# Transposed features in a ring of three 128-sample tiles: the next block's dense-table items around and between the second tile's products

## What is computed

```
e = stack([tbl_f[ids[:, f]] for f in range(26)], axis=1)   # 2048 x 26 x 128
c = concatenate([e, dense[:, None, :]], axis=1)            # 2048 x 27 x 128
z = einsum('bfd,bgd->bfg', c, c)[:, triu_i, triu_j]        # 351 pairs each
h = concatenate([z, dense], axis=1)                        # 2048 x 479
h = maximum(h @ W1 + b1, 0); h = maximum(h @ W2 + b2, 0)   # 512, then 256
y = h @ W3                                                 # 2048 x 1
```

## Time and profile before

| what | value |
|---|---|
| median of the three runs | 480.82 us |
| profiled execution, its own time | 486.82 us |
| its span, first to last instruction | 485.0 us |
| TensorE matmul / weight load busy | 437.1 us / 413.9 us |
| VectorE, ScalarE, GpSimd busy | 310.4, 230.2, 247.8 us |
| mean granted TensorE clock | 0.975 |

### The profile page before, as it was taken

The page is one execution under the profiler, slowest core; times in us unless marked ns, Lnnn a source line. Parts: engine busy times, 40 slices in busy tenths (PEclk is TensorE's granted clock), DMA queues, the critical chain, the costliest instruction groups (busy, mean ns, idle before and its releaser), DMA issues.

```text
span 485.0 us, 9121 instructions
## 1 busy us (share of the span) xinstructions
PE 437.1 (90%) x3464; PEld 413.9 (85%) x3464; DVE 310.4 (64%) x503; ACT 230.2 (47%) x731; POOL 247.8 (51%) x264
## 2 busy tenths in 40 slices
PE   1776669899998999999889999999999999999978
PEld 1665669899897999999889998989898989889966
DVE  4998237875387735885469645885488745882441
ACT  2643343644455453644545444644546453634643
POOL 3652665655655556455654656555565556461000
PEclk9999679999999999999999999999999999999999
DMA  6789212322123312232122321232133312310000
GB/s 229 222 258 160 57 45 58 81 70 72 48 63 75 81 51 57 70 82 73 44 66 78 73 65 55 70 76 78 39 72 80 80 55 56 72 49 18 1 1 0
DMA packets 23995, 36.20 MB, mean 75 GB/s; under 512 B 6185, under 2 KB 18097, under 8 KB 23952
## 3 DMA queue, kind: packets, MB, share of 16 engines
q1 hardware_dynamic: 14880, 18.03, 14.7%
q0 software_dynamic: 8192, 16.79, 12.8%
q10 hardware_dynamic: 880, 0.80, 0.5%
HBM read 35.59 MB, written 0.01 MB: 73 GB/s over the span
## 4 chain that ended last, share of the span: by engine, by line
PE 82%; DMA 7%; issue 4%; POOL 3%; DVE 2%; ACT 0%; POOLq 0%; ACTq 0%; DVEq 0%
PE x_ps L418 31%; PE gram_ps L434 24%; PE tail_ps L489 15%; DMA raw<-in_tbl,ids_sb 7%; PE x_ps L405 5%; POOL raw L388 3%; PE tail_ps L468 3%; PE tail_ps L459 2%; PE tail_ps L495 2%; DVE gram L269 1%; DVE onehot L593 1%; DMA ids_sb<-in_ids 0%; DVE z L278 0%; ACT gram L269 0%; DVE zt_lo L326 0%
## 5 line engine op out<-in xcount | busy, mean ns | idle before, releaser
L388 POOL DMA_INDIRECT raw<-in_tbl,ids_sb x256 | 246.9, 964 | 190.9 <-DMA raw<-in_tbl,ids_sb 94.6
L593 DVE TENSOR_TENSOR onehot<-ids_wide,row_ps 128x1024 fp32r<-128x1024 int32 (+1 forms) x160 | 202.6, 1298 | 41.2 <-PE x_ps L418 32.3
L418 PE MATMUL x_ps<-onehot,hot_hi 128*128 128x256 f32 x688 | 180.1, 297 | 22.2 <-DVE onehot L593 20.2
L418 PE MATMUL x_ps<-onehot,hot_lo 128*128 128x256 f32 x688 | 171.4, 283 | 0.0
L418 PEld LDWEIGHTS x_ps<-onehot,hot_hi 128*128 128x128 f32 x688 | 131.3, 191 | 26.5 <-issue 11.9
L434 PE MATMUL gram_ps<-xt 128*128 128x108 f32 x1024 | 134.2, 284 | 7.3 <-DVE gram L269 5.8
L434 PEld LDWEIGHTS gram_ps<-xt 128*128 128x128 f32 x1024 | 126.9, 199 | 13.6 <-ACT gram L269 7.6
L418 PEld LDWEIGHTS x_ps<-onehot,hot_lo 128*128 128x128 f32 x688 | 131.6, 191 | 0.0
L269 DVE COPY gram<-gram_ps 32x104 f32<-32x104 f32 x256 | 68.6, 268 | 90.2 <-PE gram_ps L434 86.3
L269 ACT COPY gram<-gram_ps 32x104 f32<-32x104 f32 x256 | 60.2, 235 | 88.7 <-PE gram_ps L434 80.1
L530 ACT COPY xt<-x_ps 128x256 f32<-128x256 f32 x80 | 50.4, 633 | 50.1 <-PE x_ps L418 42.0
(11 more groups left out here) (36 smaller groups left out, 279.0 us busy)
## 6 DMA issues: line engine op xcount, KB each, us to landing
ids_wide<-in_hot_ids SPq DMA_DIRECT2D x80, 128.0 KB
raw<-in_tbl,ids_sb POOLq DMA_INDIRECT x256
hot_in<-in_tbl SPq DMA_DIRECT2D x7, 512.0 KB, 6.8
hot_in<-in_tbl SPq DMA_DIRECT2D x3, 640.0 KB, 6.6
dense_sb<-in_dense_t ACTq DMA_DIRECT2D x6, 128.0 KB
weights_in_place<-in_w SPq DMA_DIRECT2D x1, 512.0 KB
dense_sb<-in_dense_t SPq DMA_DIRECT2D x2, 128.0 KB
weights_in_place<-in_w SPq DMA_DIRECT2D x1, 256.0 KB
```

The lines of the kernel that those rows point to most:

```text
L388: nc.gpsimd.indirect_dma_start(out=raw[k][:, f, :], out_offset=None, in_=tables[f], in_offset=bass.IndirectOffsetOnAxis(ap=ids_sb[:, t, f: ...
L418: last = nc.tensor.matmul(ps, table[:, chunk_at[j] + c, :], onehot[:, p % RING, c - a, :], start=(c == 0 and table is hot_hi), stop=(c == ...
L593: nc.vector.tensor_tensor(onehot[:, p % RING, 0:n, :], ids_wide[:, it % IDS, :].unsqueeze(1).to_broadcast([P, n, BLOCK]), row_no[chunks[it ...
```

## The change

`xt` becomes a ring of three tiles (`XT = 3`): tile t lies in place t % 3. An item of 256 samples is copied into two neighbouring places, which takes two copies where they are places 2 and 0. Block 0's hot items are made per tile, with 128 samples: 20 items of 128 columns in place of 10 of 256. A piece now holds at most 4 chunks of 256 samples or 8 chunks of 128, so the pieces of a later block become 23 (a 1250-row table has pieces of 3, 3 and 4 chunks), and block 0 has 13 for each of its tiles.

The order list is written anew. Written out for blocks 1 to 6 (t is the block's first tile):

1. the last 7 pieces of block h with the 4 turns of tile t; then the 2 pieces of item 0 of block h+1, whose copy is held back;
2. the 8 gram steps of tile t, no pieces between them; then the held item's copy;
3. 6 pieces of items 1 to 3 of block h+1, with the 4 turns of tile t+1;
4. the 8 gram steps of tile t+1 with 8 pieces of block h+1, one after each.

The tail of block h-1 is spread over the steps 1 to 3. Block 0 is: 13 pieces of tile 0 with the turns of tile 0 after its last four items; 8 gram steps of tile 0 with 8 pieces of tile 1; 5 pieces and the 4 turns of tile 1; 8 gram steps of tile 1 with 8 pieces of block 1; then the other 15 pieces of block 1, with the turns of tile 2. The last block has its grams of tile 14, then the 4 turns of tile 15, then the grams of tile 15.

Around a gram step VectorE makes at most one piece, and none right before one. The weights' split moves to the last five gram steps of block 0. SyncE loads tables two ahead in place of three, and the ids of four items of tile 1 before the weights. `h1_lo` takes the place of `h1` in SBUF.

```diff
-PIECE = 5
-EARLY = 2
+PIECE = 4
+XT = 3
+ROUNDS_AHEAD = 2
-TAIL_OVER = 3
-LOADS_AHEAD = 3
+LOADS_AHEAD = 2
-    items = blocks * nh
+    items = [(j, t, 1) for t in range(tiles_block) for j in range(nh)]
+    items += [(j, h * tiles_block, tiles_block) for h in range(1, blocks) for j in range(nh)]
...
-        count = -(-n // PIECE)
+        count = -(-chunks[j] * n * P // (PIECE * BLOCK))
...
+    def gram_slots(t, hot=()):
+        return [[("gram", t * n_gram + i)] + [step for slot in hot[i * len(hot) // n_gram:(i + 1) * len(hot) // n_gram]
+                                              for step in slot] for i in range(n_gram)]
...
+        if h == 0:
+            second = hot_pieces(1)
+            slots += gram_slots(t, second[:n_gram])
+            rest_slots = second[n_gram:]
+            slots += with_turn(rest_slots, t + 1, item_ends(rest_slots))
+            lead = 0
+        elif hot:
+            held = item_end[pieces[hot[0][0][1]][0]] - hot[0][0][1]
+            slots += hot[:held] + gram_slots(t)
+            slots[-1].append(("held", pieces[hot[0][0][1]][0]))
+            lead = n_gram
...
+        slots += gram_slots(t + 1, hot[lead:lead + n_gram])
...
+            if step[0] == "gram":
+                end = min(end, nxt + 1)
+            elif coming == ["gram"]:
+                end = nxt
...
-        xt = sb("xt", [P, BLOCK, SLOTS])
+        xt = sb("xt", [P, XT * P, SLOTS])
...
+        weights_at_gram = range(gram_block - len(weight_parts), gram_block)
...
+        def to_xt(copy, first, n, feature, src):
+            at = first % XT
+            runs = [(0, n)] if at + n <= XT else [(0, XT - at), (XT - at, n)]
+            for a, b in runs:
+                place = (first + a) % XT * P
+                last = copy(xt[:, place:place + (b - a) * P, feature], src[:, a * P:b * P])
+            return last
...
-                        last = nc.tensor.matmul(ps, table[:, chunk_at[j] + c, :], onehot[:, p % RING, c - a, :],
+                        last = nc.tensor.matmul(ps, table[:, chunk_at[j] + c, :], columns(p)[:, c - a, :],
...
-                elif kind == "xt free":
...
+                elif kind == "held":
+                    hot_copy(*what)
```

More of the change, by code:

```diff
@@ L94, in landed @@
                         if u < t or f <= upto)
[L97 removed]
+    items = [(j, t, 1) for t in range(tiles_block) for j in range(nh)]
+    items += [(j, h * tiles_block, tiles_block) for h in range(1, blocks) for j in range(nh)]
     pieces, item_end = [], []
[L99 to L102 removed]
+    for it, (j, _, n) in enumerate(items):
+        count = -(-chunks[j] * n * P // (PIECE * BLOCK))
+        cut = [i * chunks[j] // count for i in range(count + 1)]
         pieces += [(it, cut[i], cut[i + 1]) for i in range(count)]
@@ L146, in build, with hot_pieces, with_turn @@
-    first_steps = hot_steps(0, item_end[EARLY - 1])
-    order = first_steps + [step for h in range(blocks) for step in plan(h)]
+    last_item = [max(it for it, (_, first, n) in enumerate(items) if first <= t < first + n) for t in range(tiles)]
+    def hot_pieces(t):
+        of = [p for p, (it, _, _) in enumerate(pieces) if items[it][1] == t]
+        return [[("hot", p)] for p in of]
+    def with_turn(slots, t, ends):
+        for g in range(n_turn):
+            slots[ends[-(-(g + 1) * len(ends) // n_turn) - 1]].append(("turn", t, g))
+        return slots
@@ new lines, in build @@
+    held_items = [step[1] for slot in slots for step in slot if step[0] == "held"]
+    for h in range(blocks - 1):
+        at = COVER_START
+        span = [at]
+        for key, part in tail_steps[:-1]:
+            stage_ends = part == parts[key[0]] - 1 and key[1] == tail_count[key[0]] - 1
+            at += COVER_STAGE if stage_ends else COVER[key[0]]
+            span.append(at)
+        n = tail_to[h] - tail_from[h]
+        before = {}
+        for (key, part), at in zip(tail_steps, span):
+            before.setdefault(tail_from[h] + min(int(at * n / span[-1]), n - 1), []).append(("tail", h, key, part))
+        for i, steps in before.items():
+            slots[i][:0] = steps
@@ L148, in build @@
+    order = [step for slot in slots for step in slot]
     fills = [("hot", pieces[s[1]][0]) if s[0] == "hot" else s for s in order
@@ L154, in pieces_made @@
         made, nxt, used = [], 0, -1
-        for step in order:
+        for n, step in enumerate(order):
             if step[0] == "hot":
@@ L158, in pieces_made @@
             end = min(used + RING + 1, len(pieces))
+            coming = [s[0] for s in order[n + 1:] if s[0] in ("gram", "hot")][:1]
+            if step[0] == "gram":
+                end = min(end, nxt + 1)
+            elif coming == ["gram"]:
+                end = nxt
             made.append(list(range(nxt, max(nxt, end))))
@@ L252, in build, with columns @@
         row_no = {n: row_ps[:, sum(row_kinds[:i]):sum(row_kinds[:i + 1])] for i, n in enumerate(row_kinds)}
+        def columns(p):
+            it, a, b = pieces[p]
+            width = items[it][2] * P
+            return onehot[:, p % RING, 0:(b - a) * width].rearrange("p (c n) -> p c n", n=width)
+        def to_xt(copy, first, n, feature, src):
[5 more added lines that the diff above has]
+            return last
         block = ctx.enter_context(nc.Block())
@@ L363, in _ @@
                 dense_load(h)
-            for it in range(nh, items):
+            for it in range(nh + IDS, len(items)):
                 ids_load(it)
@@ L525, in hot_copy @@
             def hot_copy(it):
-                h, j = divmod(it, nh)
+                j, first, n = items[it]
                 act.wait_ge(piece_used, item_end[it])
@@ L586, in make_piece @@
                 it, a, b = pieces[p]
+                j, _, tiles_item = items[it]
+                width = tiles_item * P
                 if p == item_start[it]:
```

127 lines of the change are left out of this document (51 added, 76 removed).

## The result

The changed kernel takes 510.69 us (median of 4 runs, 507.47 to 511.16), the kernel before 481.74 (median of 4 runs, 480.33 to 486.86). The ratio is 1.0566, with a 95% interval of 1.0476 to 1.0657: **slower by 5.7%**, where 470.5 was forecast and 487 was the end of the range. The profiled execution spans 509.0 us against 485.0, 24.0 more.

The account below looks back on a forecast made before the run. TensorE was taken as the bound, 50.5 us busy and 4.7 idle a block. Turn 1.3 at 74.6, 370.9 to turn 15.3 and 29.4 to the end gave 474.9 against 485.0, thus 480.8 - 10.1, about 470.5 us; range 464 to 487.

Parts of the forecast that it names:

- Turn 0.3: Last turn of tile 0 in block 0: at 46 us (43 to 48), against 47.66 in the kernel before.
- turn 1.3: Last turn of tile 1 in block 0: at 74.6 us against 70.1, with 172 narrow matmuls at 0.11 us.
- the slow clock: Behind tile 1's last turn: about 1.6 us of lower clock goes, as TensorE is full; 0.5 left for another dip.
- The rival on narrow products: Block 0: 128-column fp32r matmuls cost 0.21 us, tile 1's last turn at 96, about 492 us in all; chance 0.18.
- From turn 1.3 to 15.3: From tile 1's last turn to tile 15's: 370.9 us against 385.5, from 353.5 of work, 15.4 idle, 1.5 and 0.5.
- The idle time by place: TensorE's idle time in a block, summed over its places: 2.2 us (1.2 to 3.6) in place of 4.7.
- The gathers take over: Rival: the last gather, landed at 441.0, sets tile 15's last turn; about 466 us; chance 0.12.
- The end: From tile 15's last turn to the kernel's end: 29.4 us, as before.
- The share of the profile: The profiled execution's gain of 10.1 us carried over to the median, 6.0 us below that execution: 480.8 - 10.1.

Follow-up runs that it names:

- experiment 3: The changed kernel with eight float32 products of 512 columns ahead of TensorE's first work: 508.05 us, ratio to the kernel before 1.0623.
- experiment 8: The changed kernel with tile 0's eight gram steps in a row ahead of tile 1's pieces: 499.94 us (one run; kernel before 493.05).
- number 6: The kernel before with block 3's hot products cut in two halves of 128 columns: 491.38 us (one run; kernel before 478.69).
- version 1: The changed kernel with block 0's hot items 256 columns wide, in the order of the other blocks: 475.62 us, ratio to the kernel before 0.9959.

## Why the prediction was wrong

- *Turn 0.3*: forecast 46 us, measured 49.4. It is no longer gathers or VectorE that set it: TensorE itself has a load every 0.213 us from 10.35 on.
- **The step that failed** is the one to turn 1.3: "I take 0.11 [...] so halving the columns can't make them dearer unless another mode sets in". The number was right at the upper level (experiment 3), and the other mode did set in: the engine's lower level. The sum to turn 1.3 has no term for it. Behind turn 1.3 the prediction even says why there would be none: "the slow clock [...] goes, since TensorE is full before it". TensorE was full, and the clock stayed down. The 172 products at 0.213 cost 17.7 us more than reckoned, the 64 gram loads 6.5 (0.213 for 0.112), turn 0.3 another 3.4, turns and copies about 1: 28.6 of the 29.2 us. The Trainium skill, in "TensorE: Matmul & The Clock Gate" under "What's actually happening", says that the clock follows how busy TensorE has been; by that, too, it would have risen. The trace doesn't agree: weight loads 20.00 us busy of 20.00 in both windows shown, and half pace.
- *The rival on narrow products* had the effect (0.21 us, turn 1.3 at 96, 492 us), but not the cause. As it is the engine and not the product that is slow, gram steps and turns pay too, which made 103.8 of its 96. The remedy differs as well: by the rival one would have to give up narrow products, in truth moving eight pieces brings turn 1.3 forward by 22 us (experiment 8).
- *From turn 1.3 to 15.3*: forecast 370.9, measured 374.5. The loads up to 110 us cost 2.3 us more (some 23 at 0.10), and stalls of 3.7 us come in block 1, where VectorE has no pieces ahead; the blocks behind give 0.5 us each back. The idle time by place, 2.2 forecast and 52.20 - 50.23 = 2.0 measured, was right for an execution that is quiet; that is luck in part, as the cause wasn't mine. The order's gram steps and turns are worth 1.7 us a block at most in the uneasy profiles, and nothing where TensorE is late or the profile is quiet (number 6); the rest of the 3.0 was the difference of two executions. What makes an execution uneasy stays open; plain copies for gathers took most of it away.
- *The gathers take over* has shown itself where the clock was repaired: in version 1 TensorE waits 11.3 us for them before turn 1.3. In the changed kernel they are off the path: the last is issued at 452.2, 26 us ahead of turn 15.3, and GpSimd waits 19.9 us for TensorE's turns where it waited 0.3.
- *The end*: 29.4 forecast, 30.7 measured.
- *The share of the profile*: I carried 10.1 us of gain over from a profiled execution that was uneasy and 6 us above its median. As the profile before was uneasy, part of this "gain" was the execution's and not the change's.

## What to carry to other kernels

Before narrowing a product at the start of a kernel, ask at which level TensorE's clock will be there. Here wide products (up at 14.7 us), half wide ones (17 us) and eight gram steps in a row (57.5 us) brought the upper level, while an engine full of narrow products and scattered gram steps stayed low for 99 us. Read the pace of one known instruction (here eight gram loads: 0.98 or 1.78 us) rather than the granted clock, above all before that record's first change. And before a stall is put down to an order, look at the longest wait for nothing visible on every engine in both profiles; where it differs, profile both kernels on one chip.

## What the runs showed of the hardware

- A stream of loads and fp32r products of 128 columns, with weight loads busy for 78.9 us of the 80 from 20 to 100, ran at the lower level (0.213 us a load, 1.2 GHz) from 10 to 109 us. With half of the products 256 columns wide the upper level came at 17 us and was lost again in a wait of 10.4 us for a gather.
- The granted clock read 1.00 over that whole stretch, and 0.50 over nearly the same one (20 to 100 us) once the clock had been up.
- Narrow products at the upper level cost 0.111 us, and transposes of 128 float32 columns 0.11; a wide product is 0.119, so halving the width saves 0.008 us.
- The kernel before took medians of 478.7 to 493.1 us on the different chips. On two of them every profile of a kernel with all its gathers has waits of GpSimd for nothing visible of up to 1.5 us or more, and TensorE, VectorE and ScalarE have such waits too. On the one where it was tried, plain copies in place of the gathers brought the blocks from 56.1 to 52.1 us.
